# A fused attention and ffn kernel: output projection two sequences behind, pairs of transposed buffers, and the first V moved

## The reference

```
n = layernorm(x)
q, k = elu(n Wq' + bq) + 1, elu(n Wk' + bk) + 1 ;  v = n Wv' + bv
num = q . cumsum(k v') ;  den = max(q . cumsum(k), 1e-6)
x = x + layernorm((num / den) Wo' + bo)
xq, s = quantise(layernorm(x))         # fp6 grid, a scale for each block of 32
x = x + layernorm((xq * s) Wf' + bf)   # Wf quantised in the same way
```

## Time and profile before

| | |
|---|---|
| median of three runs | 2392.15 us (2386.2 to 2392.42) |
| the profiled execution | 2392.45 us, its span 2390.7 us |
| granted TensorE clock, mean | 0.995 |
| PE busy | 2328.4 us, 97% of the span |
| DVE busy | 1981.4 us, 83% |
| POOL busy | 1474.0 us, 62% |
| ACT busy | 1083.8 us, 45% |

### The profile page before, as it was taken

One profiled execution on the slowest core, in us unless ns is written; L12 is line 12 of the kernel. 1 busy time (PEld: TensorE's weight loads), 2 busy tenths in 40 slices (PEclk: granted clock), 3 DMA queues, 4 the chain that ended last, 5 costly groups with the idle time before them and its releaser, 6 DMA issues.

```text
span 2390.7 us, 63829 instructions
## 1 busy us (share of the span) xinstructions
PE 2328.4 (97%) x26146; PEld 1902.4 (80%) x26146; DVE 1981.4 (83%) x3987; ACT 1083.8 (45%) x1840; POOL 1474.0 (62%) x1731
## 2 busy tenths in 40 slices
PE   7999999999999999999999999999999999999997
PEld 5878788888788788887888887888878888778885
DVE  7888788888788888888888887888888888878886
ACT  5444444444444444444444443444444444444442
POOL 4566666666566666666665665656666656656554
PEclk9999999999999999999999999999999999999999
DMA  5123222232222222222322222322123222222211
GB/s 170 60 91 100 73 83 68 75 99 87 80 71 71 91 100 73 82 67 77 99 78 90 71 69 91 99 73 82 63 82 100 73 91 73 71 91 95 77 46 36
DMA packets 108227, 195.55 MB, mean 82 GB/s; under 512 B 15136, under 2 KB 21664, under 8 KB 107424
## 3 DMA queue, kind: packets, MB, share of 16 engines
q1 hardware_dynamic: 107936, 191.47, 24.1%
HBM read 155.65 MB, written 35.78 MB: 80 GB/s over the span
## 4 chain that ended last, share of the span: by engine, by line
PE 77%; DMA 8%; ACT 4%; DVE 4%; issue 3%; POOL 2%; SPq 2%; POOLq 0%; DVEq 0%; ACTq 0%
PE work L428 11%; PE work L430 11%; PE work L429 11%; PE score L428 10%; PE score L429 10%; PE score L430 10%; PE work L550 4%; PE work L447 4%; DMA rden_dram<-rinv 4%; PE score L513 4%; DMA kc<-rden_dram 4%; PE state_bank L563 1%; POOL f_buf L1442 1%; ACT f_buf L680 1%; POOL rs_f L1388 1%
## 5 line engine op out<-in xcount | busy, mean ns | idle before, releaser
L1029 DVE TENSOR_TENSOR A<-score,causal 128x512 f32<-128x512 f32 x512 | 329.6, 682 | 21.3 <-PE score L513 21.1
L1412 POOL TENSOR_TENSOR exp_t<-exp_t,x_coef 128x512 f32<-128x512 f32 x124 | 198.3, 1599 | 141.4 <-DMA exp_t<-in_xt 141.4
L735 ACT CAST oT_hi<-kc 128x512 fp32r<-128x512 f32 x128 | 79.8, 624 | 365.0 <-DVE kc L1024 365.0
L1419 POOL TENSOR_TENSOR x_res<-x_res,o_buf 128x512 f32<-128x512 f32 x128 | 175.6, 1372 | 105.6 <-ACT o_buf L680 105.6
L428 PE MATMUL work<-wo_hi,oT_hi 128*128 128x512 f32 x512 | 204.6, 400 | 16.4 <-ACT Kn L730 13.6
L428 PE MATMUL work<-wv_hi,xT_hi 128*128 128x512 f32 x512 | 214.0, 418 | 0.7 <-issue 0.7
L1414 POOL TENSOR_TENSOR exp_t<-exp_t,x_coef 128x512 f32<-128x512 f32 x124 | 205.7, 1659 | 9.7
L428 PE MATMUL score<-xT_hi,wq_hi 128*128 128x512 f32 x512 | 206.8, 404 | 2.1 <-DVE KT L969 2.1
L428 PE MATMUL score<-xT_hi,wk_hi 128*128 128x512 f32 x512 | 205.9, 402 | 0.7 <-DVE xT_lo L960 0.7
L429 PE MATMUL work<-wv_lo,xT_hi 128*128 128x512 f32 x512 | 201.1, 393 | 0.8 <-issue 0.8
L430 PE MATMUL work<-wv_hi,xT_lo 128*128 128x512 f32 x512 | 201.8, 394 | 0.0
(11 more groups left out here) (134 smaller groups left out, 6394.9 us busy)
## 6 DMA issues: line engine op xcount, KB each, us to landing
x_in<-in_x SPq DMA_DIRECT2D x128, 256.0 KB, 4.5
kc<-rden_dram SPq DMA_DIRECT2D x128, 256.0 KB
x_res<-in_x SPq DMA_DIRECT2D x128, 256.0 KB, 2.8
exp_t<-in_xt SPq DMA_DIRECT2D x124, 256.0 KB, 3.0
out<-f_buf SPq DMA_DIRECT2D x96, 256.0 KB, 2.0
x_coef<-coef_dram SPq DMA_DIRECT2D x31, 512.0 KB, 3.6
out<-xd SPq DMA_DIRECT2D x32, 256.0 KB, 2.1
rden_dram<-rinv SPq DMA_DIRECT2D x32, 64.0 KB, 3.4
```

Of the source, the lines that this page charges most:

```text
L1029: nc.vector.tensor_tensor(A[:, j, :, :], score_bank[j][:], causal[:].unsqueeze(1).to_broadcast([P, G, P]), ALU.mult).then_inc(a_set, 1)
L1412: nc.gpsimd.tensor_tensor(rows, rows, by_token(0), ALU.mult).then_inc(x_scaled, 1)
L1419: nc.gpsimd.tensor_tensor(x_res[:, b, :], x_res[:, b, :], o_buf[:, b % 2, :], ALU.add).then_inc(r_set, 1)
```

## The change

Four things are changed together, and the lists of all five engines are written anew around them.

- On PE `o` stands two sequences behind its attention: `o(i,0)` between `v(2)` and `attend(2)`, `o(i,1)` between `v(3)` and `attend(3)`, `o(i,2)` and `o(i,3)` behind `k(0)` and `k(1)` of the next turn. Nothing stands between `v(1)` and `attend(1)` any more.
- On PE `v(0)` stands between `past_products` and `denominators`.
- The transposed inputs of o and of xd share two pairs of buffers, T_hi0/T_lo0 and T_hi1/T_lo1; before, o had only the first pair and xd both.
- x is loaded two turns ahead instead of one, and SP's list is interleaved otherwise. The banks are given out anew.

```
-    (("o", 3), W1), (("xd", 0), W0), (("f", 0), W2), (("xd", 1), W1), (("f", 1), W0),
...
+    (("v", 0), W1), (("kn", 0), W0), (("f", 3), W1), (("att", 0), W2), (("kn", 1), W0),
+    (("v", 1), W1), (("att", 1), W0), (("kn", 2), W1), (("v", 2), W2), (("o", 0), W1),
+    (("att", 2), W2), (("kn", 3), W0), (("v", 3), W1), (("o", 1), W0), (("att", 3), W1),
...
-    if name in ("xd", "f") or stage == ("o", 3):
+    if name in ("xd", "f") or stage in (("o", 2), ("o", 3)):
...
+        xdT_hi = oT_hi = [T_hi0[:], T_hi1[:]]
+        xdT_lo = oT_lo = [T_lo0[:], T_lo1[:]]
...   SP, inside a turn
+                after = i + 2 < TILES
                 if prev:
                     store(i - 1, 0)
+                if after:
+                    load_x(i + 2, 0)
+                    load_x(i + 2, 1)
...
                 if cur:
                     store_rden(i)
                     spread_rden(i, 0)
+                if prev:
+                    store(i - 1, 1)
...   PE
                 k(0)
                 if prev:
+                    o(i - 1, 2)
+                k(1)
+                if prev:
                     o(i - 1, 3)
                 xd_transposes(0)
-                k(1)
                 k(2)
+                k(3)
                 f(0)
-                k(3)
...
                 past_products()
+                v(0)
                 denominators()
-                v(0)
...
                 v(1)
-                if cur:
-                    o(i, 0)
                 attend(1)
```

More of the change, by code:

```diff
@@ L368, in turn @@
                     spread_coef(i + 1)
[L369 to L372, removed]
+                if after:
+                    load_x(i + 2, 2)
                 if nxt:
@@ L378, in turn @@
                     spread_rden(i, 0)
+                if prev:
+                    store(i - 1, 1)
+                if cur:
                     spread_rden(i, 1)
+                if nxt:
+                    load_xt(i + 1, 2)
+                if cur:
                     spread_rden(i, 2)
+                if prev:
+                    store(i - 1, 2)
+                if cur:
+                    load_res(i, 0)
+                if nxt:
+                    load_xt(i + 1, 3)
+                if cur:
                     spread_rden(i, 3)
                 if prev:
-                    store(i - 1, 2)
-                if prev and cur:
-                    load_res(i, 2)
[L386 to L391, removed]
+                    store(i - 1, 3)
+                if after:
+                    load_x(i + 2, 3)
+                if cur:
+                    load_res(i, 1)
+                    load_res(i, 2)
                     load_res(i, 3)
-                if not prev:
-                    for b in range(NSEQ):
-                        load_res(i, b)
             def load(dst, src, signal):
@@ L415, in _ @@
                 load(dst[:], src.to_broadcast([P, D]), small_loaded)
+            for b in range(NSEQ):
+                load_x(1, b)
             turn(0, False, True, True)
@@ L1272, in turn @@
+                scale(i - 1, 2)
+                f_seen(0)
+                if nxt:
+                    widen(i + 1, "x", 3)
+                join(i - 1, "f", 0)
+                quantise(i - 1, 2)
+                phi_k(3)
+                widen(i - 1, "f", 0)
+                phi_q(0)
                 greatest(i - 1, 3)
                 scale(i - 1, 3)
[L1274 to L1275 removed]
+                scan(2)
+                phi_q(1)
                 quantise(i - 1, 3)
[L1277 removed]
@@ L1303, in turn @@
                 mask(0, 3)
+                if nxt:
+                    x_lo(i + 1, 0)
                 f_bias(3)
-                normalise(0)
-                o_lo(0)
-                f_seen(3)
                 mask(1, 0)
                 mask(1, 1)
-                join(i - 1, "f", 3)
-                v_bias(1)
+                f_seen(3)
                 mask(1, 2)
                 mask(1, 3)
+                v_bias(1)
+                if nxt:
+                    x_lo(i + 1, 1)
+                normalise(0)
@@ L1338, in turn @@
+                mask(3, 2)
+                mask(3, 3)
+                v_bias(3)
+                r_seen(i, 0)
+                join(i, "r", 0)
+                if nxt:
+                    x_lo(i + 1, 3)
                 widen(i, "r", 0)
                 o_lo(2)
-                mask(3, 2)
-                if nxt:
-                    x_lo(i + 1, 2)
-                mask(3, 3)
+                o_bias(i, 1)
+                o_seen(i, 1)
+                normalise(3)
+                join(i, "o", 1)
```

446 lines of the change are left out of this document (208 added, 238 removed).

## The result

The changed kernel takes 2401.68 us (median of 17 runs, 2396.1 to 2407.49), the one before 2392.15 us in runs on the same chip (2386.2 to 2398.82). The ratio is 1.0042, with a 95% interval from 1.0032 to 1.0053: slower by a little more than the 0.3% that a measurement can tell. The forecast was 2383 us, faster; the time lies inside the range of 2373 to 2403, on the wrong side of it.

What follows compares the result with a forecast made beforehand. PE's stream of matmuls was taken as the bound. 31 turns of 72.78 us make 2256.2, 11.1 less than 2267.3; with 2 us for the ends the span is 2381.6, with 1.75 around it 2383; eight in ten within 2373 to 2403.

Steps and rivals of the forecast that it cites:

- The new wait: attend(1) on PE waits for V(1) with its bias, no longer covered by o(0): 0.83 us a turn, 25.7 us.
- The clock did not fall for it: Rival: attend(1)'s new wait lets PE's clock fall, 1.5 us in each of 31 turns, 2429 us; chance 0.02.
- o two sequences behind: Moving o on PE removes its 13.6 us of waits for the Kn copy and 3.6 us of attend's mask waits.
- the rival at 2411: Sequence 3's Kn copy, behind o(0)'s norm on ACT, makes o(1) wait 0.9 us a turn, 28 us; chance 0.12.
- 71.80: Length in us of the shortest turn before the change, taken as a turn without waits; the mean was 73.14.
- V(0) between the small products: V(0) parts PE's run of 320 small instructions: 9.4 us of instruction waits go, and 3 us of half clock.
- the forecast's 72.78: Forecast steady turn in us: 71.80 + 0.83 + 0.15, the last for remaining instruction waits and small collisions.
- the instruction waits only move: Rival: PE's late-instruction waits shift place, so the 9.4 and 3 us stay, 2395 us; chance 0.11.
- The two ends: First and last turn together take 2 us longer, bounds -2 and +6.
- The contention with POOL: Rival: DVE's x_lo(1), slowed beside POOL's x_scale, delays V(2) beyond 2 us of slack: 15 us, 2398 us; chance 0.09.
- the single row: Profile row before: DVE's oT_lo took 2.15 us, usually near 0.69, beside a POOL product; 1.46 us lost, fitting the slack.

Runs made afterwards that it cites:

- e3: The changed kernel with scores(2) moved from behind state(1) to between V(1) and attend(1) in every turn; 2380.27 us, ratio 0.9964.
- e5: The kernel before with V(0) alone moved between the products with the state and the denominators, in every turn; 2393.52 us, ratio 1.0012.
- e1: The changed kernel with only the lists of the first turn altered (Wf's low parts and the next turn's x_lo earlier); 2399.33 us, ratio 1.0042.
- e2: The changed kernel with only the last turn's lists altered: residual's norm of sequence 1 ahead of the norm of o(2); 2401.53 us, ratio 1.0051.
- e6: The changed kernel with the lists of the first and last turn written anew, the 30 turns between untouched; 2385.87 us, ratio 0.9982.
- e8: The changed kernel with the state products parted, 96 matmuls ahead of V(0) and 32 behind, in every turn but the first; 2415.57 us, ratio 1.0105.

## Why the prediction was wrong, by its steps

- **The new wait**, 0.83 us in each of 31 turns, 25.7 us: right to the tenth, and e3 shows its cause. The clock did not fall for it.
- **o two sequences behind**: what it forecast came. The 13.6 us of waits for Kn are gone and so are the masks' waits in the steady turns, and no wait of o(1) for the copy behind the norm came (the rival at 2411). The shortest turn after is 72.63 us, as 71.80 + 0.83 says. That it was o's move that did it is shown in part only: with V(0) moved alone (e5) the waits for Kn fell to 6.7 us and those for the masks from 5.3 to 2.0, and no run has o's move, or the new list of SP, by itself.
- **V(0) between the small products**: right in kind, too high in its gain. I let one stop of 0.9 us stay and took 0.15 us a turn for all that is left. In the profiled execution there were three in the products (2.70, 1.49, 1.32) and one at V (1.59), with half clock behind the first, and the turns' mean is 73.04, 0.41 above the shortest, not 0.15. That is 7.8 us too much in 30 turns. Of the 12.3 us above the shortest, the four turns with a stop hold 9.9, and turn 1, right behind the first, 1.6. The same steady lists ran in e1, e2 and e6 with means of 72.87, 72.91 and 72.78, which is 0 to 4 us over the forecast's 72.78. The rival "the instruction waits only move" was right for a part: they come with 109 or more records of small matmuls in a row, and the products alone have 128. e8, without stops, has all but two turns within 0.07 us of one another, so little else was in this residual. The cause of a stop, that instructions come late, is still argued and not shown.
- **The two ends, 2 us with bounds of -2 and +6: this is the step that failed.** By the windows they cost 17 us. The forecast's 30 turns of 72.78 are 2183.4 us, which leaves 198.2 of its span of 2381.6 for the two end windows, 4.5 more than before (the windows part the time otherwise than the marks of the earlier trace rows, hence not 2); measured are 210.8. For the first turn I wrote that o(2) is gone and that V(0) stands ahead of what it must wait for, "about the same". V(0)'s wait alone is 3.36 us, and the half clock behind it makes V(0) take 4.54 us, 1.6 more than the usual 2.95; and I never followed the chain of x (`x_scale`, `x_hi`) through the first turn's own lists, where POOL does the norm of o(0) ahead of it and attend(3)'s seed waits for it, 3.87 us. For the last turn I named the right cause, the later norms of sequence 1, and gave it no size of its own: xd(1)'s transposes wait 3.74 us, and the waits of the last stretch add up to 13.3 us against 9.4 before. e6 shows that it was the lists and nothing that the change must have: with others the ends are 3.5 us longer than before by the windows (83.87 for 84.43, 113.32 for 109.31), within the 4.5 forecast.
- **The contention with POOL**: the contention came, the wait of V(2) did not. In 18 of the 30 steady turns `x_lo(1)` takes 1.25 to 2.04 us instead of 0.69, and always ends 0.55 us behind a product of `x_scale` that POOL had begun first; the 2 us of slack covered it, as the single row had said. In e3, where V(2) comes sooner, it reached PE. In two turns the two began within 0.03 us of each other: then DVE took its 0.69 us and POOL's product 2.1 instead of some 1.6. Two turns of the changed kernel, DVE and POOL of each:

```profile
444.99 2.03 DVE L965 TENSOR_TENSOR xT_lo<-exp_t,xT_hi 128x512 fp32r<-128x512 f32 x1
```

```profile
444.92 1.55 POOL L1418 TENSOR_TENSOR exp_t<-exp_t,x_coef 128x512 f32<-128x512 f32 x1 [0.72 <-DMA exp_t<-in_xt]
```

```profile
1027.91 0.69 DVE L965 TENSOR_TENSOR xT_lo<-exp_t,xT_hi 128x512 fp32r<-128x512 f32 x1
```

```profile
1027.94 2.08 POOL L1418 TENSOR_TENSOR exp_t<-exp_t,x_coef 128x512 f32<-128x512 f32 x1 [0.81 <-DMA exp_t<-in_xt]
```

The span of 2402.0 us is 20.4 over the forecast's 2381.6: 12.6 of it lie in the two ends and 7.8 in the turns between. In e1 and e2, with the same steady lists, the turns between are 2.8 and 3.8 us over the forecast, in e6 they are on it. So it is the ends that turned the sign: with e6's the ratio is 0.9982 and the time 2385.87 us, near the 2383 forecast.

## What to carry to other kernels

A pipeline that is moved by a stage has three prices: the steady turn, the first and the last. The shortest steady turn can be right to 0.01 us and be outweighed by 8 to 10 us at each end, where a list of its own decides; so each chain that ends at PE (loads too) is followed through the first and last lists separately, and the ends are given bounds as wide as the single waits seen there. When a piece of work is taken from between a producer and its reader, something else that is free at that time goes in its place: 1.1 us of scores gave back 19 us here.

## What the hardware showed that I had not expected

- The stops called "issue" come late in a run of small matmuls: but for the start of turn 0, every stop in the products has 109 or more records ahead of it in all ten profiled executions, and the run of 96 has none in 31 turns. They can also fall a little behind the run: inside V in four executions, and once (e1, 0.65 us) behind V and 13 records of the denominators. The places recur from one execution to the next (in the changed kernel behind 126 records in turn 4, 120 in turn 13, 115 in turn 22, 128 in turn 24; e1 and e2, with the same steady lists, stop at two and three of these); the length differs, from nothing to 2.7 us. This fits packets of 254 instructions whose ends drift through the turn, which no run tests. The Trainium skill ("Advanced Engine Details and Errata", ISA Cache) gives lines of 256 instructions, with which the packets agree. Its 128 KB on TensorE would, taken as a full store, carry a run of 320; if the stops are late instructions, it was not full then.
- Four row groups side by side are not four times one: 14 ns a record on four, 15 on three, 31 on one. The 31 hold the change from V and to the denominators; inside that run four records start every 109 ns, 27 each. The Trainium skill ("TensorEngine Tiling (Array Packing)", Key Properties) says that tiles work independently; the 32 matmuls on one row group still had four column groups among them, so the rows show only the factor of about 2 (31 or 27 to 14) between one row group and four.
- Waits of 0.83 us in each turn and one of 1.49 left matmuls at 0.39 us behind them, those of 2.87 to 3.87 had a stretch at 0.63. The length of the last wait does not decide alone: behind one of 2.45 us (at 33.13) the matmuls stay at full clock, and behind two of 2.05 and 1.26 us (at 59.18 and 61.07) they do not. The granted clock's mean in the first stretch is 0.93 after and 0.96 before and in e6.
